# Cross-attention, gated-cell and expert block on one core: gate constants and both cell norms on ScalarE, and the second batch's quotient ahead of the first batch's residual norm

## The reference

```python
# end of the first sublayer (audio = layernorm(x))
attn_out = attn_num / attn_denom
attn_out = attn_out @ Wo.T + bo
return _layernorm(audio + attn_out, gamma, beta)
...
# the gated cell; its x is layernorm(x), and its steps are the two batches
c0 = jnp.broadcast_to(in_c, (batch, in_c.shape[0]))
def step(c, xt):
    ft = jax.nn.sigmoid(xt @ wf.T + c @ uf.T + bf)
    it = jax.nn.sigmoid(xt @ wi.T + c @ ui.T + bi)
    gt = jnp.tanh(xt @ wc.T + c @ uc.T + bc)
    c = ft * c + it * gt
    return (c, None)
c_final, _ = lax.scan(step, c0, x)
h = jnp.tanh(jnp.einsum('tbi,oi->tbo', x, wo) + c_final @ uo.T + bo)
return h
```

## Time and profile before

| what | value |
|---|---|
| median of 3 executions | 180.94 us (179.95 to 181.54) |
| the profiled execution, its own time | 182.35 us |
| its span in the trace | 180.5 us, so 1.85 us lie around it |
| TensorE busy | 163.2 us (90%) |
| VectorE busy | 118.7 us (66%) |
| ScalarE busy | 102.9 us (57%) |
| GpSimd busy | 73.0 us (40%) |

### The profile page before, as it was taken

One profiled execution on the slowest core, in us unless ns is written; L12 is line 12 of the kernel. 1 busy time (PEld: TensorE's weight loads), 2 busy tenths in 40 slices (PEclk: granted clock), 3 DMA queues, 4 the chain that ended last, 5 costly groups with the idle time before them and its releaser, 6 DMA issues.

```text
span 180.5 us, 2419 instructions
## 1 busy us (share of the span) xinstructions
PE 163.2 (90%) x712; PEld 96.3 (53%) x712; DVE 118.7 (66%) x380; ACT 102.9 (57%) x185; POOL 73.0 (40%) x120
## 2 busy tenths in 40 slices
PE   1999998979885799999999999999999899999992
PEld 1554655434332348555655644367667566677781
DVE  3758898984367488866568557666769664566541
ACT  3446638846753324899747577673664446645621
POOL 2399272262372043976621041352522244322500
PEclk9999999999999966999999999999999999999999
DMA  6798600000000234300000000000000000001001
GB/s 177 264 315 178 210 8 0 2 0 2 2 0 0 57 75 101 77 0 0 0 4 0 0 0 0 4 0 2 0 5 0 0 0 0 0 0 58 4 0 58
DMA packets 5570, 7.23 MB, mean 40 GB/s; under 512 B 749, under 2 KB 3606, under 8 KB 5558
## 3 DMA queue, kind: packets, MB, share of 16 engines
q1 hardware_dynamic: 5142, 6.66, 13.0%
q10 hardware_dynamic: 416, 0.42, 0.7%
HBM read 5.17 MB, written 0.52 MB: 32 GB/s over the span
## 4 chain that ended last, share of the span: by engine, by line
PE 65%; DVE 18%; ACT 8%; issue 4%; POOL 2%; DMA 1%; SPq 0%; DVEq 0%; POOLq 0%; ACTq 0%
PE bank L1120 7%; PE bank L1156 6%; PE bank L1268 5%; PE bank L1175 4%; PE bank L1270 4%; PE bank L1269 4%; PE bank L1251 3%; PE bank L1253 3%; PE bank L1252 3%; PE bank L1178 3%; DVE stats L1325 3%; PE bank L1237 3%; PE bank L914 2%; PE bank L1196 2%; POOL rstd L526 2%
## 5 line engine op out<-in xcount | busy, mean ns | idle before, releaser
L644 POOL TENSOR_TENSOR pair<-early,pair 128x512 fp32r<-128x512 f32 x16 | 20.5, 1287 | 38.6 <-ACT pair L861 38.6
L1600 DVE SCALAR_TENSOR_TENSOR pair<-bank,pair 128x512 fp32r<-128x512 f32 x32 | 21.6, 690 | 19.0 <-ACT pair L868 18.9
L1512 DVE TENSOR_REDUCE nmax<-bank 128x2 f32<-128x308 f32 x64 | 26.3, 471 | 11.4 <-PE bank L1120 11.2
L836 ACT ACTIVATE prob<-bank 128x512 f32<-128x512 f32 x40 | 22.7, 597 | 6.4 <-PE bank L1156 6.1
L1120 PE MATMUL bank<-pair,q_s 97*128 97x308 f32 x64 | 22.1, 411 | 0.7 <-ACT q_s L813 0.3
L868 ACT ACTIVATE pair<-bank 128x512 fp32r<-128x512 f32 x32 | 18.8, 596 | 6.1 <-PE bank L1253 4.8
L861 ACT ACTIVATE pair<-early 128x512 fp32r<-128x512 f32 x16 | 10.1, 632 | 21.1 <-DVE early L1596 21.1
L526 POOL TENSOR_TENSOR rstd<-vare,m_half 128x4 f32<-128x4 f32 x10 | 10.4, 1044 | 24.4 <-DVE vare L1330 21.1
L1120 PEld LDWEIGHTS bank<-pair,q_s 97*128 97x128 f32 x64 | 13.2, 214 | 12.0 <-DVE nmax L1512 7.1
L1156 PE MATMUL bank<-q_s,pair 112*128 112x512 f32 x40 | 17.5, 452 | 0.1
L1268 PE MATMUL bank<-pair,w_h 128*128 128x512 f32 x32 | 14.1, 440 | 0.0
(11 more groups left out here) (239 smaller groups left out, 314.0 us busy)
## 6 DMA issues: line engine op xcount, KB each, us to landing
w_s<-in_w SPq DMA_DIRECT2D x1, 1024.0 KB, 7.3
prob<-in_w SPq DMA_DIRECT2D x1, 1024.0 KB, 12.8
q_s<-q_late SPq DMA_DIRECT2D x12, 64.0 KB, 2.0
q_s<-pair SPq DMA_DIRECT2D x9, 64.0 KB, 2.0
x_t<-in_x SPq DMA_DIRECT2D x2, 256.0 KB, 3.1
wf_s<-in_w_ffn SPq DMA_DIRECT2D x1, 512.0 KB, 4.8
row<-in_rows SPq DMA_DIRECT2D x1, 260.0 KB, 3.9
wc_s<-in_w_ctx ACTq DMA_DIRECT2D x1, 256.0 KB, 4.1
```

What stands on the lines that cost most here:

```text
L644: pool.tensor_tensor(ec_l[:, n % NEC], ec[:, n % NEC], ec_h[:, n % NEC].bitcast(F32), ALU.subtract).then_inc(ec_lo, 1)
L836: nc.scalar.activation(prob[:, u % NPR], bank[ST[u % 3]][:], ACT.Exp).then_inc(prob_ready, 1)
L1512: dve.tensor_reduce(nmax[:, b, q, j, g:g + 2], item_bank("score", n)[:, 0:2 * TK].rearrange("p (h k) -> p h k", k=TK), AX.X, ALU.max, nega ...
L1600: dve.scalar_tensor_tensor(out=hid_l[:, g % NH], in0=bank[RING[g % 4]][:], scalar=0.0, in1=hid_h[:, g % NH].bitcast(F32), op0=ALU.max, op1 ...
```

## The change

VectorE computes `quotient(1)` ahead of `residual_norm(0)`. ScalarE writes all four tiles of both z_n norms, and VectorE's two calls of `ln_apply` for them are gone, as is TensorE's wait for VectorE in `turn_z`. The three columns of `gate0` are written by ScalarE, ahead of `keys_of(0)`, from TensorE's product with `gate1` as bias; `gate1` and `c0_half` are written by VectorE early in its program. The two names C_BF and C_BI are neighbouring columns.

```diff
@@ scalar
+            act.wait_ge(gate_c_mm, 1)
+            act.wait_ge(gate_c_ready, 1)
+            for g in range(3):
+                nc.scalar.activation(gate0[:, g:g + 1], bank[1][:, g:g + 1], ACT.Identity, bias=gate1[:, g:g + 1],
+                                     scale=1.0 if g == 2 else 0.5).then_inc(gate_c_done, 1)
+            act.wait_ge(gate_c_done, 3)
             act.wait_ge(head_ready, 1)
             act.wait_ge(kf_ready, 1 + len(K_PAIRS))
...
-            normalise(LN_X1, 0, lambda b, j: x1[:, b, j], z_n, z_ready_act)
+            normalise(LN_X1, 0, lambda b, j: x1[:, b, j], z_n, z_ready_act, 0)
...
-                    normalise(LN_X1, 1, lambda b, j: x1[:, b, j], z_n, z_ready_act)
+                    normalise(LN_X1, 1, lambda b, j: x1[:, b, j], z_n, z_ready_act, 0)
@@ tensor
             def turn_z(b):
-                pe.wait_ge(z_ready, b + 1)
                 pe.wait_ge(z_ready_act, b + 1)
...
-            pe.wait_ge(gate_c_ready, 1)
+            pe.wait_ge(gate_c_done, 3)
@@ vector
             dve.tensor_scalar(bq0_neg[:], col[:, C_BQ0:C_BQ0 + 1], -1.0, None, ALU.mult).then_inc(bq0_ready, 1)
+            dve.tensor_scalar(gate1[:, 0:2], col[:, C_BF:C_BF + 2], 0.5, None, ALU.mult)
+            dve.tensor_copy(gate1[:, 2:3], col[:, C_BC:C_BC + 1])
+            dve.tensor_scalar(c0_half[:], col[:, C_INC:C_INC + 1], 0.5, None, ALU.mult).then_inc(gate_c_ready, 1)
...
-            def gate_constants():
...
             centred(0)
+            quotient(1)
             residual_norm(0)
-            quotient(1)
-            ln_apply(LN_X1, 0, x1, z_n, NJ_DVE).then_inc(z_ready, 1)
-            gate_constants()
             residual(1)
             centred(1)
             residual_norm(1)
             cell_gates(0)
-            ln_apply(LN_X1, 1, x1, z_n, NJ_DVE).then_inc(z_ready, 1)
             cell_out(0)
```

More of the change, by code:

```diff
@@ L310, in two_blocks @@
         gate_c_ready = sem("gate_c_ready")
+        gate_c_done = sem("gate_c_done")
         a_ready = sem("a_ready")
```

## The result

| | median | executions |
|---|---|---|
| changed kernel | 183.86 us | 6, 181.74 to 187.43 |
| kernel before, beside it | 181.24 us | 6, 179.75 to 183.96 |
| ratio | 1.0143, 95% interval 1.009 to 1.0196 | |

The change made the kernel slower by 1.4%; the forecast was 181.1 us, with a range up to 183.2.

What follows compares the result with a forecast made beforehand. It took VectorE's chain up to batch 1's transposes as the bound; its 1.05 us gain is eaten by ScalarE's longer norms, net +0.17 to +0.2. 180.94 + 0.2 = 181.1 us; own range 180.3 to 182.1, widened to 180.1 to 183.2.

Steps and rivals of the forecast that it cites:

- a gain of 1.05: VectorE, freed of norm tiles and constants, starts batch 1's statistics at 30.2 instead of 31.26, 1.05 us earlier.
- the sum: Net delay of batch 1's transposes: +0.50 and +0.76 through batch 0, 0.57 lost as slack, +0.76 again: +0.17 to +0.2 us.
- the start of batch 1's norm, 0.57 earlier: ScalarE starts batch 1's norm behind the third tanh, at 37.66 instead of 38.23.
- the two tiles more, 0.76: ScalarE writes four norm tiles per batch instead of two, in series, adding 2 x 0.38 = 0.76 us per batch.
- the three constants: Gate constants on ScalarE ahead of the key layout at 28.88: 0.36 us, hidden by later factors; upper end 1.15.
- rival 1: TensorE's clock falls in the new 2.1 us gap before batch 0's transposes: 182.8 to 185 us, middle 183.5; chance 0.17.
- the thin one: TensorE's thinly busy window from 58 to 60 us, 0.89 of 2 us, before the trace's one clock fall.
- 0.6 us what two medians can stand apart: Three runs lay within 1.6 us, so two medians could stand 0.6 apart with no change.

Runs made afterwards that it cites:

- the third run: The changed kernel timed again with no edit, for more executions and another trace: 183.89 us, ratio 1.0133 to the kernel before.
- the three groups: Twelve follow-up runs in groups of four, each on one chip with its own 23, 29 or 35 executions of the kernel before: medians 182.06, 182.12, 181.10 us.
- the one with the gap: The kernel before without the four and two filler products on either side of batch 1's projection: 182.39 us, ratio 1.0103.

## Why the prediction was wrong

Its working on the order of the work held to within 0.15 us. Predicted and measured: second quotient 26.4 (26.40); batch 1's statistics at 30.2 (30.07), a gain of 1.05 (1.2); ScalarE's norm of batch 0 from 31.04 (31.07); its transposes at 32.8 (32.77); gate products at 34.2 (34.20); norm of batch 1 directly behind the third tanh at 37.66 (37.64), transposes at 39.4 (39.33). At equal clock the changed kernel is 0.0 to 0.1 us longer in the stage of the change, where the sum said +0.17 to +0.2. (That sum can't be added up as its last sentence writes it. What it rests on is the start of batch 1's norm, 0.57 earlier, plus the two tiles more, 0.76.)

One term was off without effect. I took 0.36 for the three constants, from activations without a bias column:

```profile
28.74 0.55 ACT L762 ACTIVATE gate<-bank,gate 128x1 f32<-128x1 f32 x3
29.33 1.36 ACT L771 ACTIVATE pair<-q_s,head_of 112x1280 fp32r<-112x1280 f32 x1
```

The key layout began 0.45 later than before (29.33 for 28.88). With that ScalarE was ready at the moment the factors came (31.03), so it cost nothing. The estimate from the Trainium skill's price (ScalarE: Activation LUTs, What ACT_TABLE_LOAD costs) was 0.56 for three, so the measured delay lies between the two; one such activation lasted 254 to 265 ns, where I estimate 281 by the page's formula.

The step that failed is the weight of rival 1: the sum put the clock at nothing, and the rival had a chance of 17%. Its mechanism and its place were right: the gap was 2.31 us (2.1 forecast), and in the third run's trace the clock fell behind it at 34.3. Its price was not: it gave 2 to 4 us for the fall, and the fall cost 1.70. That the median, 183.86, lies near its 183.5 is luck, because the rest came from a low stretch behind 58 us that it had not priced (1.3 us in one trace, 2.4 in another). What failed is the sentence "Against it: the low stretch came 4 us after the thin one, and behind the new gap TensorE works without a break." Work behind the pause did not save the clock; in both traces with a fall it came in the midst of the gate products. I had held the pause against the one thin stretch of a single trace and found it shorter, as if that trace were the limit of what the clock bears. The kernel's own three times, 1.6 us apart with a profiled execution above them all, already said that something in it varied by the microsecond, and I booked that as noise around the median instead of asking what it was. The range ended at 183.2, inside this case's own 182.8 to 185.

It was also wrong to call 0.6 us what two medians can stand apart: the kernel before's medians in the three groups, of 23 to 35 executions each, were 182.06, 182.12 and 181.10.

## What to carry to other kernels

A change that frees one engine can open a pause on another; ask of each pause on TensorE whether it gets longer in one piece, and fill it before timing the change. Where executions differ, sort their times by the mean granted clock: equal times at equal clocks and another spread of clocks point to the clock and not to the order of the work. Then cut the traces into stages, because the mean doesn't say where the clock was low, and the same low time cost 1.70 us in one place and 0.6 in another. One trace is one draw; here the profiled execution was the best of six and did not show the fall in the new pause.

## What the runs showed of the hardware

The clusters at 179.6, 181.1, 183.1 and 185.8 us, all at a mean clock of 0.995 or more, come from the first 20 us. There the granted clock reads full, but TensorE's products take nearly twice as long in some executions as in others. The same product of batch 0's queries, in the kernel before and in the version with the quotient alone:

```profile
9.86 2.08 PE L957 MATMUL bank<-a_f,w_s 128*128 128x512 f32 x2
```
```profile
9.53 1.12 PE L957 MATMUL bank<-a_f,w_s 128*128 128x512 f32 x2
```

and the numerator's product in the kernel before and in the one with the gap:

```profile
15.20 1.12 PE L979 MATMUL bank<-q,kv 128*128 128x512 f32 x2
```
```profile
16.07 2.08 PE L979 MATMUL bank<-q,kv 128*128 128x512 f32 x2
```

A product of 2.08 us for 1.12 is what a granted clock of half makes elsewhere (749 ns for 409). The slow products last from the start up to some point between 9 and 19 us that differs from execution to execution, while the windows there show 1.00: the mean clock of a result doesn't count this time. The first column of the table by stages bears out that the clusters are such points: it is 18.7 to 18.9 in the two traces of the shortest cluster, 19.6 to 20.5 in eleven, and 22.25 in the one at 183.21. No trace fell on the cluster at 185.8, and what sets the point wasn't tried.
